# Four attention layers on one core: engine orders from a list schedule, self-attention pairs between cross pairs, the 8-bit layer's clamps on GpSimd and its takes on two engines, x loaded first

## Chip, cores, metric

One core of a Trainium2 chip. The time is that of one execution of the program on the device, in microseconds (us); the median of several runs is used for comparisons. TensorE (PE) runs at a granted clock: 1.00 in the profile is 2.4 GHz, 0.50 is 1.2 GHz.

## What is computed

`x` is 32 sequences of 112 tokens of 256 channels, `ctx` is 32 sequences of 375 tokens of 256 channels. Four layers follow one another on x, each attending to ctx with 16 heads, everything in float32:

```python
x = L0(x, ctx)   # rmsnorm of x and of ctx, cross-attention, 4 key/value heads of 64, residual
x = L1(x, ctx)   # layer norm, self-attention, layer norm, cross-attention, gated FFN (exact gelu);
                 # heads of 16; q, k, v and the softmax weights rounded to 8 bits:
                 #   xq = clip(round(x / delta) + zp, 0, 255); (xq - zp) * delta
x = L2(x, ctx)   # layer norm, cross-attention, 16 heads of 64, FFN of 1024 (relu)
x = L3(x, ctx)   # layer norm, causal self-attention, cross-attention, FFN of 1024; heads of 16
```

## The kernel before

**Tiling.** Channels lie on the partitions, tokens along the free axis. A *stream* is two sequences (224 tokens); a layer has 16 streams. A stream's x is read from DRAM into one of five buffers at the start of a layer and stored at its end; contexts come one sequence at a time into two buffers. All weights of a layer lie in SBUF.

**Attention.** A *unit* is one head of cross-attention (112 x 375 scores) or four heads of self-attention (112 x 448). A *pair* is two units; an *octet* is four cross pairs (eight heads of a sequence) or two self pairs (all sixteen heads). Layers 0 and 2 have 256 cross pairs; layers 1 and 3 have 256 cross and 64 self pairs. A pair goes through these steps:

- scores: PE, line 937, into two of four PSUM banks; waits for the exp of the pair two before
- max: DVE, line 1215; in layer 1 also the product with a scale, nmaxc, line 1219
- exp: ACT, line 1106, one instruction (and one read of its sum) for each unit, or for each head in a self unit; writes `e`, which holds four pairs, so it waits for the turns of the pair four before
- invert: DVE, line 1226; in layer 1 also rsumw, line 1230
- weigh: POOL (GpSimd), lines 1431 (layer 1) and 1434, in place in `e`
- turn: PE transposes, line 950 (cross) and 947 (self), into a bank of the ring
- take: a copy from PSUM to `probs`, on DVE (1295) or ACT (1120); in layer 1 always DVE (1293), where it takes off the rounding constant and applies the bound 255
- pv: PE, lines 975, 982, 989, 964, once for an octet; its save is DVE's.

**Jobs.** Every other matrix product is a *job*: norms (mean, var), q, k, v, context keys and values (ck, cv), output products (o, o2), FFN (f1, gate, up, f2). Jobs, turns and pvs use a ring of four PSUM banks in the order of PE's queue; job n waits for the save of job n - 4. The products run from line 1000. In layer 1 a quantised product (q, k, v, ck, cv; 16 a stream) is saved by ACT (line 1142: scaled and rounded, into one of four tiles of `work`), clamped by DVE (line 1264) and, right behind it and with a wait for it, unpacked by DVE (*clip*, lines 1271 to 1282). ACT's save of product n waits for the clip of product n - 4.

**Order of work.** A Python planner (`Plan`) writes out every engine's queue before the program is built. Each step has a hand-given *position*, counted in pairs: a turn comes 2.35 positions after its scores (2.85 for self-attention), an FFN job so many after its stream's last pair. `arrange` sorts PE's steps by position and keeps that order; a running clock with estimated costs then gives every other step a due time, and DVE, ACT, POOL and SP execute theirs sorted by due time. A step marked "VA" goes to whichever of DVE and ACT is free earlier. All queues run in order, tied by semaphores. In layers 1 and 3 the self pairs of stream s + 1 stand among the cross pairs of stream s as whole octets: self, cross, self, cross, cross, cross, so two self pairs follow one another.

**Start.** SP loads constants, four vectors of parameters and the causal mask, then (by due time) the three weight parts that are free at once (3.25 MB of layer 0, layer 1's early part and layer 2's v), then x, two contexts and so on. DVE makes scales and masks (lines 1368 to 1400) in a chain; ACT waits for it (`setup_done`) before its first instruction on data.

## Time and profile before

| what | value |
|---|---|
| median of 3 runs | 5542.59 us (5533.66 to 5542.77) |
| the profiled execution, its own time | 5541.59 us |
| its span, first to last instruction | 5539.8 us |
| mean granted clock of PE | 0.957 |
| instructions | 90952 |

In the page's 40 slices PE's granted clock is lowest in slices 9 to 18 and PE's busy share in slices 1 and 8 to 18:

```profile
PE   8999999888888888889999999999999999999999
...
PEclk9999999988888888889999999999999999999999
```

Each digit is a tenth of a slice of 138.5 us; 9 is 90% or more. Layer 0 runs to about 990 us, layer 1 to 2490, layer 2 to 4150, layer 3 to the end. A busy PE is not a PE at its peak: matmul ends are modelled. An engine's idle time costs nothing where the engine isn't what the end waits for.

### The profile page before, as it was taken

The page shows a single profiled execution, that of the slowest core. Times are in us where ns is not written, and L with a number is a line of the kernel's source. Part 1 is how long each engine was busy: PE and PEld are TensorE (multiplying, and loading weights), DVE is VectorE, ACT ScalarE, POOL GpSimd, SP SyncE. Part 2 cuts the span into 40 slices and gives each one's busy share as a digit, 9 for nine tenths or more (in the row PEclk, how much of TensorE's full clock was granted, in tenths as well). Part 3 has the DMA queues.
Part 4 walks back from the last instruction along what each step waited for, and adds up shares of the span by engine and source line. Part 5 has one row for each costly group of instructions (what it writes and reads, how often), then busy time and mean ns, then how long its engine had stood idle before and what let it go on. Part 6 is the DMA issues. An engine that isn't in the chain of part 4 may idle for free.

```text
span 5539.8 us, 90952 instructions
## 1 busy us (share of the span) xinstructions
PE 5246.6 (95%) x34496; PEld 3760.9 (68%) x34496; DVE 3463.5 (63%) x7972; ACT 2652.3 (48%) x8353; POOL 1559.0 (28%) x3090
## 2 busy tenths in 40 slices
PE   8999999888888888889999999999999999999999
PEld 5666666566667676666666666666677777777777
DVE  5555555677777777775455555555556666666665
ACT  4555555666665666653232232223234555555554
POOL 2332322333332323332111111111113333333332
PEclk9999999988888888889999999999999999999999
DMA  1000000100000000000100000000000100000000
GB/s 71 19 19 25 21 19 17 43 13 10 19 10 16 13 10 19 10 31 14 36 13 10 15 12 10 16 12 10 14 21 19 36 16 13 19 19 11 19 18 9
DMA packets 39746, 103.05 MB, mean 19 GB/s; under 512 B 4880, under 2 KB 21520, under 8 KB 38032
## 3 DMA queue, kind: packets, MB, share of 16 engines
q1 hardware_dynamic: 39312, 97.23, 5.3%
q8 instruction: 276, 4.52, 0.3%
q14 instruction: 158, 1.29, 0.1%
HBM read 82.53 MB, written 14.68 MB: 18 GB/s over the span
## 4 chain that ended last, share of the span: by engine, by line
PE 83%; DVE 8%; ACT 5%; POOL 2%; issue 1%; DMA 0%; SPq 0%; ACTq 0%
PE ring L1000 49%; PE score L937 13%; PE ring L950 11%; ACT e L1106 3%; PE ring L982 3%; PE ring L975 3%; DVE nmax L1215 3%; PE ring L947 2%; PE ring L989 1%; DVE probs L1293 1%; POOL e L1431 1%; POOL e L1434 1%; DVE nmaxc L1219 1%; PE ring L964 1%; DVE values L1282 1%
## 5 line engine op out<-in xcount | busy, mean ns | idle before, releaser
L1434 POOL TENSOR_SCALAR e<-e,rsum 112x375 f32<-112x375 f32 (+1 forms) x2048 | 1065.9, 536 | 2922.7 <-DVE rsum L1226 2921.3
L1106 ACT ACTIVATE e<-score,nmax 112x375 f32<-112x375 f32 (+1 forms) x2048 | 1041.1, 528 | 655.6 <-DVE nmax L1215 651.9
L1215 DVE TENSOR_REDUCE nmax<-score 112x2 f32<-112x750 f32 (+1 forms) x1152 | 1099.1, 954 | 325.3 <-PE score L937 312.2
L950 PEld LDWEIGHTS ring<-consts,e 112*125 112x125 f32 x6144 | 821.1, 192 | 328.7 <-issue 188.6
L950 PE MATMUL ring<-consts,e 112*125 112x112 f32 x6144 | 920.1, 284 | 84.3 <-POOL e L1431 41.5
L1000 PE MATMUL ring<-h,weights 128*128 128x224 f32 x3840 | 951.1, 377 | 16.6 <-ACT h L1084 12.8
L1000 PEld LDWEIGHTS ring<-h,weights 128*128 128x128 f32 x3840 | 708.5, 199 | 166.7 <-issue 62.4
L937 PE MATMUL score<-keys,q 64*112 64x375 f32 (+2 forms) x3584 | 788.0, 505 | 2.7 <-DVE q L1271 1.1
L1431 POOL TENSOR_SCALAR e<-e,rsumw 112x375 f32<-112x375 f32 (+1 forms) x1024 | 480.8, 488 | 1027.3 <-DVE rsumw L1230 1026.4
L1106 ACT ACTIVATE e<-score,nmaxc,quant 112x375 f32<-112x375 f32 (+1 forms) x1024 | 555.3, 564 | 367.7 <-DVE nmaxc L1219 367.0
L1120 ACT COPY probs<-ring 125x336 f32<-125x336 f32 (+1 forms) x716 | 301.0, 440 | 729.6 <-PE ring L950 718.4
L1000 PE MATMUL ring<-weights,ctx 128*125 128x256 f32 (+1 forms) x1536 | 570.2, 502 | 0.5 <-DVE probs L1293 0.5
L1000 PE MATMUL ring<-ctx,weights 128*128 128x375 f32 x1536 | 559.7, 486 | 9.5 <-DVE work L1345 6.8
L1295 DVE COPY probs<-ring 125x336 f32<-125x336 f32 (+1 forms) x948 | 471.1, 517 | 91.0 <-PE ring L950 72.0
L937 PEld LDWEIGHTS score<-keys,q 64*112 64x112 f32 (+2 forms) x3584 | 245.4, 165 | 331.8 <-issue 249.1
L1106 ACT ACTIVATION_READ_ACCUMULATOR e<-score,nmax 112x1 f32 x2048 | 438.4, 214 | 0.0
L1000 PE MATMUL ring<-work,weights 128*128 128x224 f32 (+1 forms) x1792 | 403.9, 374 | 2.4 <-DVE work L1251 1.7
L1000 PE MATMUL ring<-heads,weights 128*128 128x224 f32 x1536 | 367.6, 386 | 31.1 <-ACT work L1142 30.7
L1000 PEld LDWEIGHTS ring<-ctx,weights 128*128 128x128 f32 x1536 | 275.2, 191 | 174.6 <-issue 57.0
L1000 PEld LDWEIGHTS ring<-weights,ctx 128*125 128x125 f32 x1536 | 284.4, 192 | 149.5 <-issue 104.0
L1000 PEld LDWEIGHTS ring<-work,weights 128*128 128x128 f32 x1792 | 328.1, 190 | 44.8 <-issue 8.2
L1000 PEld LDWEIGHTS ring<-heads,weights 128*128 128x128 f32 x1536 | 301.8, 205 | 79.8 <-ACT work L1142 33.8
(105 smaller groups left out, 5193.7 us busy)
## 6 DMA issues: line engine op xcount, KB each, us to landing
ctx<-ctx_t SPq DMA_DIRECT2D x128, 375.0 KB, 3.0
out_t<-x SPq DMA_DIRECT2D x64, 224.0 KB, 2.0
x<-out_t SPq DMA_DIRECT2D x48, 224.0 KB, 3.2
weights<-weights SPq DMA_DIRECT2D x5, 1024.0 KB, 4.8
x<-x_t SPq DMA_DIRECT2D x16, 224.0 KB, 3.2
weights<-weights SPq DMA_DIRECT2D x1, 3328.0 KB, 10.9
weights<-weights SPq DMA_DIRECT2D x1, 2560.0 KB, 8.8
weights<-weights SPq DMA_DIRECT2D x1, 2304.0 KB, 9.1
```

Of the source, the lines that this page charges most:

```text
L937: ins = pe.matmul(score_bank(u)[0:S, n * width:(n + 1) * width], lhs, rhs, start=not masked, stop=not masked or n == nt - 1)
L947: ins = pe.transpose(dst[0:S, n * S:(n + 1) * S], src[:, n * S:(n + 1) * S], idt[0:S, 0:S])
L950: ins = pe.transpose(dst[0:R, c * S:(c + 1) * S], src[:, c * R:(c + 1) * R], idt[0:S, 0:S])
L975: ins = pe.matmul(ps[64 * odd:64 * odd + 64, 0:4 * S], vs[0:R, c, kv:kv + 64], probs_of(o, c, 4 * odd, 4 * S), start=c == 0, stop=c == last)
L982: ins = pe.matmul(ps[64 * odd:64 * odd + 64, i * S:(i + 1) * S], vs[0:R, c, hd:hd + 64], probs_of(o, c, 4 * odd + i, S), start=c == 0, sto ...
L1000: ins = pe.matmul(out_, a, b_, start=n == 0, stop=n == len(parts) - 1)
L1106: ins = nc.scalar.activation(e_of(u)[:, n * width:(n + 1) * width], score_bank(u)[0:S, n * width:(n + 1) * width], ACT.Exp, bias=minus, sc ...
L1120: ins = nc.scalar.copy(dst, src)
L1215: ins = dve.tensor_reduce(to, src, AX, ALU.max, negate=True)
L1295: ins = dve.tensor_copy(dst, src)
L1431: ins = nc.gpsimd.tensor_scalar(mine, mine, rsumw[0:S, slot(u), n:n + 1], ROUND, ALU.mult, ALU.add)
L1434: ins = nc.gpsimd.tensor_scalar(mine, mine, rsum[0:S, slot(u), n:n + 1], 0.0, ALU.mult, ALU.add)
```

## The change

1. **Orders.** Every step on PE (T), DVE (V), ACT (A), POOL (G) and SP's queue (D) becomes a `Step` with a cost, a position and a list of what must come before. `arrange` plays the program through: whenever an engine is free it takes, of its steps whose inputs are done, the one with the smallest position. PE may take only steps up to 6 positions past its first open one, and no job while the ring is full. That order is written into the queues. Semaphore counts follow from it (`nth`).
2. **Self pairs** stand singly between the cross pairs of the first two cross octets: c s c s c c, twice. Turns come 2.2 positions after their scores for both kinds, pvs 0.5 after that (0.9 before, with 2.35 and 2.85).
3. **Layer 1's clamps** move from DVE to POOL, in the order ACT save, POOL clamp, DVE clip; the clip waits for `clamped` and is no longer chained to an instruction before it.
4. **Layer 1's takes** may go to ACT (Identity with bias -ROUND) as well as DVE (subtract ROUND, without the minimum). For this the bound 255 goes to the weighing, and the rounding constant is added in a second pass of POOL over the same `e`, one instruction a unit, which waits for the first pass; turns wait for it (`gridded`).
5. **nmaxc and rsumw** become products of two tensors (with `scales`, filled at setup) in place of a tensor and a per-partition scalar. Setup has three more instructions for each of two sets, and two more memsets on POOL.
6. **Start.** Layer 0's weights come in three parts (q; k and v; o), with positions after x's; the early parts of layers 1 and 2 no longer go first.

```diff
-    (0, ("q", "k", "v", "o"), 0),
+    (0, ("q",), 0),
+    (0, ("k", "v"), 2048),
+    (0, ("o",), 3072),
...
-                for at, o in zip(places, own):
-                    cross.insert(at, o)
-                for o in cross:
-                    self.octet(*o)
+                    places = (0, 1)
+                for i, o in enumerate(cross):
+                    o = self.octet(*o)
+                    beside = self.octet(*own[places.index(i)]) if own and i in places else None
+                    for n in range(4):
+                        self.pair(o)
+                        if beside and n < 2:
+                            self.pair(beside)
...
+            self.add("weigh", p, "G", (2.7 if own else 1.15) + ((1.3 if own else 1.1) if q else 0), p.index + 1.0)
...
+                self.add("clamp", j, "G", 0.55 if j.kind in ("ck", "cv") else 0.4, j.pos + 0.3)
+                self.add("clip", j, "V", self.clip_cost(j), j.pos + 0.5)
...
+            first = {0: -10.5, 1: -10.9, 2: -4.0, 3: 20.0}.get(i, 60.0)
+            self.add("weights", i, "D", 8.0, max((j.pos for j in js), default=first) + 0.3)
...
+    def arrange(self):
+        engines = ("T", "V", "A", "G", "D")
...
+        while left:
+            for e in engines:
+                if free[e] > now:
+                    continue
...
+                if e == "T":
...
+                    full = len(self.ring) >= RING and self.ring[-RING] not in released
+                    open_ = [w for w in waiting["T"] if w.pos <= undone[behind].pos + AHEAD
+                             and not (full and w.kind == "job")]
+                else:
+                    open_ = waiting[e] + (waiting["VA"] if e in "VA" else [])
+                if open_:
+                    step = min(open_, key=place)
...
+                step.end = now + cost
+                free[e] = now + (0.3 if e == "D" else cost)
+                self.order[e].append((step.kind, step.x))
...
+                events += [(free[e], serial, None), (step.end + 0.1, serial + 1, step)]
...
+                if layer == 1:
+                    rows = S if is_own(j.of.octet) else R
+                    ins = nc.scalar.activation(dst, src, ACT.Identity, bias=minus_magic[0:rows, :])
...
-                        ins = dve.tensor_scalar(nmaxc[0:S, pair_slots(p), 0:nt], to, quant[0:S, a + 4:a + 5], None, ALU.mult)
+                        ins = dve.tensor_tensor(nmaxc[0:S, pair_slots(p), 0:nt], to, scale_of(o, 0), ALU.mult)
...
-            chained(dve.tensor_scalar(r, r, ROUND + 127.0, ROUND - 128.0, ALU.min, ALU.max))
...
-                    ins = dve.tensor_scalar(dst, src, ROUND, 255.0, ALU.subtract, ALU.min)
+                    ins = dve.tensor_scalar(dst, src, ROUND, None, ALU.subtract)
...
+                if kind == "clamp":
+                    rows, width = quantised_shape(x_)
+                    r = rounded[0:rows, x_.place % 4, 0:width]
+                    wait.saves([x_])
+                    nc.gpsimd.tensor_scalar(r, r, ROUND + 127.0, ROUND - 128.0, ALU.min, ALU.max).then_inc(clamped, 1)
+                    continue
...
-                            ins = nc.gpsimd.tensor_scalar(mine, mine, rsumw[0:S, slot(u), n:n + 1], ROUND,
-                                                          ALU.mult, ALU.add)
+                            ins = nc.gpsimd.tensor_scalar(mine, mine, rsumw[0:S, slot(u), n:n + 1], 255.0,
+                                                          ALU.mult, ALU.min)
...
+                if o.layer == 1:
+                    wait.wait_ge(weighed, nth["weigh", p])
+                    for u in p.units:
+                        mine = e_of(u)[:, 0:count_of(o) * width]
+                        ins = nc.gpsimd.tensor_scalar(mine, mine, ROUND, 0.0, ALU.add, ALU.add)
+                    ins.then_inc(gridded, 1)
```

## Rows read from the trace of the kernel before

**Rows 1.** The page's part 1: busy us of each engine (share of the span) and instructions.
```profile
PE 5246.6 (95%) x34496; PEld 3760.9 (68%) x34496; DVE 3463.5 (63%) x7972; ACT 2652.3 (48%) x8353; POOL 1559.0 (28%) x3090
```

**Rows 2.** Busy time by stage: stretch, length, engines, granted clock, DMA share, GB/s.
```profile
0.00:25.00 25.00, 4.41 (x9) 3.09 (x10) 7.73 (x38) 3.56 (x6) 2.65 (x9) 1.00 0.73 283
25.00:990.00 965.00, 963.15 (x5024) 612.10 (x5023) 547.53 (x1107) 504.60 (x1496) 287.14 (x497) 1.00 0.07 21
990.00:2490.00 1500.00, 1265.56 (x8260) 992.95 (x8260) 1135.60 (x3099) 917.77 (x2680) 485.11 (x1027) 0.85 0.05 16
2490.00:4150.00 1660.00, 1656.57 (x9594) 1124.67 (x9594) 859.47 (x1679) 510.40 (x1532) 295.91 (x514) 1.00 0.05 16
4150.00:5500.00 1350.00, 1326.36 (x11397) 1001.27 (x11400) 901.41 (x2025) 708.93 (x2626) 484.45 (x1038) 1.00 0.06 18
```

**Rows 3.** The same view: one repeat of layer 1 and its stretches at 0.50.
```profile
1606.55:1702.12 95.57, 80.91 (x529) 64.26 (x530) 72.33 (x199) 58.74 (x170) 30.04 (x64) 0.84 0.04 14
1606.55:1623.62 17.07, 10.61 (x61) 7.47 (x61) 11.55 (x31) 10.08 (x41) 7.79 (x21) 0.50 0.07 23
1637.27:1644.10 6.83, 6.45 (x40) 4.32 (x39) 5.31 (x15) 6.41 (x25) 2.09 (x7) 0.50 0.00 0
1661.17:1668.00 6.83, 6.21 (x19) 5.77 (x20) 4.80 (x16) 3.68 (x10) 2.33 (x4) 0.50 0.00 0
```

**Rows 4.** Waits of PE, 990 to 2490 us: total us, times, longest us.
```profile
PE ring L947 <- POOL e L1431: 53.3, 17, 3.5
PE ring L950 <- POOL e L1431: 41.5, 47, 2.3
```

**Rows 5.** The chain of waits, 1606 to 1625 us: start us, us, what.
```profile
1608.90 2.34 ACT e L1106 x11
...
1614.82 2.70 POOL e L1431 x8
...
1617.66 1.71 PE ring L947 x8
```

**Rows 6.** Groups of instructions: busy us, mean ns of one, idle before; POOL's by form.
```profile
L1431 POOL TENSOR_SCALAR e<-e,rsumw 112x375 f32<-112x375 f32 x512 | 304.6, 607 | 816.3 <-DVE rsumw L1230 816.0
L1431 POOL TENSOR_SCALAR e<-e,rsumw 112x112 f32<-112x112 f32 x512 | 176.8, 368 | 211.0 <-DVE rsumw L1230 210.4 <-DVE rsum L1226 0.6
...
L1215 DVE TENSOR_REDUCE nmax<-score 112x2 f32<-112x750 f32 (+1 forms) x1152 | 1099.1, 954 | 325.3 <-PE score L937 312.2
L1106 ACT ACTIVATE e<-score,nmax 112x375 f32<-112x375 f32 (+1 forms) x2048 | 1041.1, 528 | 655.6 <-DVE nmax L1215 651.9
L1293 DVE TENSOR_SCALAR probs<-ring 125x336 bf16<-125x336 f32 (+1 forms) x640 | 315.5, 525 | 46.0 <-PE ring L947 36.6 <-PE ring L950 6.7
L1120 ACT COPY probs<-ring 125x336 f32<-125x336 f32 (+1 forms) x716 | 301.0, 440 | 729.6 <-PE ring L950 718.4 <-PE ring L947 9.9
L1264 DVE TENSOR_SCALAR work<-work 128x224 f32<-128x224 f32 (+4 forms) x256 | 85.6, 334 | 92.6 <-ACT work L1142 92.3
```

**Rows 7.** Waits of PE, 4150 to 5500 us.
```profile
PE ring L947 <- POOL e L1434: 19.4, 15, 1.4
```

**Rows 8.** The timeline of the start: start us, us, instruction, idle before it.
```profile
3.53 1.38 SPq L1477 DMA_DIRECT2D weights<-weights  x3
4.96 0.50 SPq L1457 DMA_DIRECT2D x<-x_t  x1
...
13.14 0.46 DVE L1400 TENSOR_SCALAR qbias<-vectors,qmask 128x1 f32<-128x1 f32 x2
19.87 0.58 ACT L1073 ACTIVATE squares<-x 128x448 f32<-128x448 f32 x1 [17.86 <-DMA x<-x_t]
```

**Rows 9.** The page's part 6, DMA issues: count, KB each, median us to landing.
```profile
x<-x_t SPq DMA_DIRECT2D x16, 224.0 KB, 3.2
```

**Rows 10.** Two lines of DVE: duration ns as min/median/max, first and last start us.
```profile
L1275 DVE TENSOR_SCALAR keys<-work x32: 276/552/605, 946.3 to 2333.1; 128x224 bf16<-128x224 f32 x32
...
L1219 DVE TENSOR_SCALAR nmaxc<-nmax,quant x320: 227/228/1874, 981.5 to 2527.6; 112x2 f32<-112x2 f32 x128, 112x8 f32<-112x8 f32 x32
```

More of the change, by code:

```diff
@@ L104 @@
     half: int
-    first: int = 0
-    last: int = 0
+    pairs: tuple = ()
 @dataclass(eq=False)
@@ L135 @@
     nth: int = 0
-    clip: int = 0
-    norm: int = -1
+    pos: float = 0.0
+    norm: object = None
+    place: int = 0
 @dataclass(eq=False)
@@ L149, in mm, with __init__ @@
     return count * n / 600.0
+class Step:
+    def __init__(self, kind, x, by, cost, pos):
+        self.kind, self.x, self.by, self.cost, self.pos = kind, x, by, cost, pos
+        self.then, self.left, self.end = [], 0, None
 class Plan:
@@ L205, in span, with octets_of @@
+            if p is o.pairs[-1] and len(o.pairs) == (2 if o.attn == "self" else 4):
+                self.pv_of[o] = self.job(p.index + lag + 0.5, "pv", o.layer, o.s, o.b, o.half, PV_BY, o)
+    def octets_of(self, layer, attn, s):
+        return [o for o in self.octets if (o.layer, o.attn, o.s) == (layer, attn, s)]
     def span(self, layer, attn, s):
-        os = [o for o in self.octets if (o.layer, o.attn, o.s) == (layer, attn, s)]
-        return os[0].first, os[-1].last + 1
+        os = self.octets_of(layer, attn, s)
+        return os[0].pairs[0].index, os[-1].pairs[-1].index + 1
@@ L421, in clock_of @@
         for layer in range(4):
+            for b in range(B):
+                first = [j.pos for j in self.jobs if j.layer == layer and j.b == b and j.kind in ("cvar", "ck", "cv")]
+                self.add("ctx", (layer, b), "D", 4.0, min(first) - 2.5)
             for s in range(STREAMS):
-                sync.append((one(layer, "f2" if layer else "o", s, 0, 1) + 1.0, "store", (layer, s)))
+                self.add("store", (layer, s), "D", 2.0, self.at[layer, "f2" if layer else "o", s, 0, 1].pos + 0.5)
@@ L442, in clock_of @@
                 user = (32 if layer == 1 else 128) + slot
-                j = self.products(user - VS)[-1]
-                pool.append((ends[j] + 3.0, "zero", (layer, slot, j)))
-        j = self.at[1, "pv", last, B - 1, 0]
-        own = [i for i in self.ring if i.kind == "pv" and i.layer == 1 and i.of.attn == "self"]
-        pool.append((ends[own[-1]] + 40.0, "zero_own", own[-1]))
-        self.pool = [x[1:] for x in sorted(pool, key=lambda x: x[0])]
+                self.add("zero", (layer, slot), "G", 0.8 if layer == 1 else 1.6,
+                         self.value_users(user - VS)[-1].pos + 1.0)
@@ new lines, in before_save @@
+    def before_save(self, j):
+        yield "job", j
+        if j.kind == "turn":
+            o = j.of.octet
+            if o.index >= 2:
+                yield "job", self.pv_of[self.octets[o.index - 2]]
+        elif j.kind == "mean":
+            yield from self.h_free(j.norm)
+        elif j.kind == "var":
+            if j.norm.index >= 2:
+                yield "scale", self.norms[j.norm.index - 2]
+        elif j.kind == "cvar":
+            if j.b:
+                yield "cscale", j.b - 1
+        elif not (j.layer == 1 and j.kind in QUANTISED):
+            yield from self.frees(j)
@@ new lines, in ready, with query_jobs, key_jobs, value_jobs @@
+    def ready(self, j):
+        return ("clip" if j.layer == 1 and j.kind in QUANTISED else "save"), j
+    def query_jobs(self, o):
+        return self.every(o.layer, "q2" if o.layer in (1, 3) and o.attn == "cross" else "q", s=o.s)
+    def key_jobs(self, o):
+        if o.attn == "self":
+            return self.every(o.layer, "k", s=o.s)
+        return [j for j in self.every(o.layer, "ck", b=o.b) if o.layer != 2 or j.m // 4 == o.half]
+    def value_jobs(self, o):
+        if o.attn == "self":
+            return self.every(o.layer, "v", b=o.b)
+        return [j for j in self.every(o.layer, "cv", b=o.b) if o.layer != 2 or j.m // 3 == o.half]
@@ L762, in done @@
                 self.wait_ge(job_done, max([j.index for j in jobs], default=-1) + 1)
-        every = plan.every
-        last_s = STREAMS - 1
-        turns = {j.of: j for j in plan.ring if j.kind == "turn"}
-        pv_of = {j.of: j for j in plan.ring if j.kind == "pv"}
-        def turned_input(wait, p):
-            wait.wait_ge(weighed, p.index + 1)
+        every, nth = plan.every, plan.nth
+        eight_bit = [x_ for k_, x_ in plan.order["G"] if k_ == "weigh" and x_.octet.layer == 1]
+        grid_count = {p: i + 1 for i, p in enumerate(eight_bit)}
@@ L898, in tensor_program @@
             wait.wait_ge(consts_loaded, 16)
-            wait.wait_ge(consts_made, 6)
-            for kind, x_ in plan.tensor:
+            wait.wait_ge(consts_made, 8)
+            for kind, x_ in plan.order["T"]:
                 if kind == "scores":
@@ L955, in tensor_heads @@
             layer = o.layer
-            wait.saves([turns[u] for p in plan.pairs[o.first:o.last + 1] for u in p.units])
+            wait.saves([plan.turn_of[u] for p in o.pairs for u in p.units])
+            wait.products(plan.value_jobs(o))
             last = CHUNKS - 1
             if is_own(o):
-                wait.products(every(layer, "v", b=o.b))
                 for half in range(2):
@@ L968, in tensor_heads @@
                 return ins
-            wait.products([i for i in every(layer, "cv", b=o.b) if layer != 2 or i.m // 3 == o.half])
             vs = cross_values(layer, o.b, o.half)
```

788 lines of the change are left out of this document (469 added, 319 removed).

## The prediction

> **What bounds the kernel now.** I read the page's busy line first: PE is busy 95% of the span [rows 1]. The table by stage says where the rest is [rows 2]. Layer 0 (25 to 990 us) and layer 2 (2490 to 4150 us) have PE busy for 963.15 of 965 us and 1656.57 of 1660 us at a granted clock of 1.00; no order of work can give anything there. Layer 3 has 23.6 us of PE idle time in 1350 us, the start 20.6 us. Layer 1 (990 to 2490 us) has 234 us of idle PE and a granted clock of 0.85: it pays twice, with idle time and with busy time at the lower clock. So I cut one stream's repeat of layer 1 along the clock [rows 3]. It lasts 95.57 us (the pattern comes back at this distance through the layer, so 1500 us are 15.7 repeats). PE is busy 80.91 us, of which 10.61 + 6.45 + 6.21 = 23.27 us lie in the three stretches at 0.50 (1.2 GHz). At 2.4 GHz those would be about 11.6 us, so PE's own work is 57.6 + 11.6 = 69.3 us. The difference, 26 us in each repeat or 410 us in all, is the most that layer 1 can give.
>
> Why PE stops: its waits in layer 1 are led by the turns (transposes) of weighed scores, on POOL [rows 4]. The chain through the largest gap shows what feeds it [rows 5]: two self-attention pairs in a row put sixteen exps on ACT (a piece of eleven of their instructions takes 2.34 us), then come eight weighings on POOL (2.70 us), and only then does PE turn. No other engine is full in this repeat: DVE 72.3 us, ACT 58.7, POOL 30.0 of 95.6 [rows 3]. It is latency in a fixed order, made worse by bunching, and by the clock that falls when PE has starved.
>
> **The change, part by part, for one repeat of layer 1** (16 cross pairs, 4 self pairs, 16 quantised products).
>
> PE: not one matmul is added or removed. 69.3 us stays.
>
> POOL: the weighing is now two passes, the second being one instruction per unit: 32 of 375 wide and 8 of 448 wide. A 375-wide one takes 0.607 us, a 112-wide one 0.368 [rows 6]; the line through both gives 0.67 us at 448. So 32 x 0.607 + 8 x 0.67 = 24.8 us. The clamps are 16 instructions of 224 to 512 wide, which the same line puts at 0.47 to 0.73 us: about 8.7 us. Each second pass also waits for the first to drain, which no row shows; between 0 and 0.3 us (the largest gap between two engines in the chain is 0.2), I take 0.15, so 3 us for 20 pairs. POOL goes from 30.0 to about 66.5 us.
>
> DVE: the clamps go, 85.6 us / 16 = 5.3 us [rows 6]. nmaxc and rsumw are still 40 small instructions, with two tensors in place of a tensor and a scalar: no cost taken; bounds below. 72.3 - 5.3 = 67 us. ACT stays at 58.7. The takes (315.5 us / 16 = 19.7 us for 40, all DVE's now) may go to either; a copy of such a tile costs ACT 0.440 us, and that is the price I take there [rows 6]. Shared evenly, (67 + 58.7)/2, both carry about 63 us, with some 9 takes moved.
>
> So at the floor of 69.3 us PE would be full and three engines 90% to 96% full. Four in-order queues don't all run at that. The orders are worked out from estimated costs in which an engine hears of another's end after 0.1 us. The self pairs are split up, which takes the bunch out of ACT and POOL, and PE may choose among steps up to six positions ahead, so most of the 14.7 us of idle time should go. But a self pair's weighing grows from 2.7 to some 4.2 us, and a cross pair's from 1.2 to 2.4 us, on the very path PE waits for. The bounds are 69.3 us (all gained) and 95.6 us (nothing). Layer 3 keeps PE 98% busy, but with DVE at 67%, ACT 53% and POOL 36% [rows 2]; layer 1 before has 85% with DVE at 76%. I take 88% to 90% of PE's 69.3 us, 78 us, and 2 us for stretches still at 1.2 GHz: **80 us a repeat**. 15.7 x 15.6 = **245 us gained**.
>
> Layers 0 and 2: 5.3 us of PE idle in 2625 us. The new order can only lose here. A pair there takes 965/256 = 3.8 us and 1660/256 = 6.5 us of PE, so a turn 2.2 positions later comes 8 or 14 us after its scores, and the chain (maximum 0.95, two exps 1.1 and the last of their sums, two weighings 1.2 [rows 6], five handovers of up to 0.2) is under 5 us: it is covered. I take 5 us lost, bounds 0 and 40 (1.5%).
>
> Layer 3: 19.4 of its 23.6 us of PE waiting are turns of self pairs on POOL [rows 7]. Spreading these pairs removes the bunch, but the turn's distance for self pairs falls from 2.85 to 2.2. I take 12 us gained, bounds 24 gained and 15 lost.
>
> Start: the first x is issued at 4.96 us behind three weight transfers, and its square starts at 19.87 us [rows 8]. With x issued first, at about 3.5 us, and landing 3.2 us later [rows 9], the bound becomes the vector constants: the setup ends at 13.6 us now, and ACT waits for it [rows 8]. Six more links of about 0.25 us each make 15.1 us. Gain 19.9 - 15.3 = 4.6, say 5 us, if the weights for q (1 MB, behind x, context and k, v) are down by 19 us. Bounds 0 and 6. The tail, from the last pair to the store, is a chain of single steps: unchanged. What else is moved on SP's queue (loads, stores and the weights now in 13 parts for 11) comes in a stage whose DMA share is 0.04 to 0.07 [rows 2], and I take nothing for it.
>
> Sum: 245 - 5 + 12 + 5 = 257 us. The profiled execution took 5541.59 us (span 5539.8, 1.8 us around it), the median of the runs is 5542.59, 1 us more. 5541.6 - 257 = 5284.6; I forecast **5285 us**.
>
> **Rivals.**
> (A) PE is nearly filled. Repeat of 70 to 75 us, nothing left at 1.2 GHz. For it: each loop has buffers for it (four pairs in e, two in score banks). Against: three other engines over 85%. Gain 20.6 to 25.6 x 15.7 = 323 to 402 us, plus 12: 5130 to 5207 us. Chance 0.15.
> (B) DVE and POOL get in each other's way. The row that speaks for it: the clips of k take 276 ns at best and 552 ns at the median, the same instruction on the same shape, with POOL busy 31% of this time, and nmaxc reaches 1874 ns over a median of 228 [rows 10]. Against: for nmaxc the median is the minimum plus 1 ns. If about 76 DVE instructions a repeat (40 small products, 30 clips, 6 scalings) meet a POOL busy at 85% and wait for half of a 0.6 us instruction, that is 76 x 0.85 x 0.3 = 19 us. DVE carries 82 us, and the repeat becomes 87 to 92 us: gain 55 to 135 us, plus 12; 5395 to 5475 us. Chance 0.15. The Trainium skill, in SBUF — State Buffer, "Who interferes with whom", says that a DVE instruction with two SBUF inputs, as the new nmaxc and rsumw are, or in a two-port mode, shuts out a GpSimd instruction that reads SBUF and the reverse, for the whole instruction. By that rule this case, not mine, is to be expected; the medians there agree with it for one kind of clip alone.
> (C) Slower. ACT's queue is held by POOL's. ACT may save quantised product n only when product n - 4 is clipped, and that now needs POOL's clamp, which can stand behind a weighing of 4.2 us. Behind the waiting ACT stand all exps. Sixteen such waits a repeat at 2.5 us would bring ACT to 63 + 40 = 103 us: 7.4 x 15.7 = 116 us lost, 5650 us. It decides from (95.6 - 63)/16 = 2.0 us a wait. Against: the new order puts a save only after its clip is due. Chance 0.06.
> (D) The fixed order, built from estimates, mismatches the chip everywhere: all layers lose 1% to 2%, layer 1 gains little; near 5540 us. Chance 0.04.
>
> **How the numbers follow.** Forecast 0.60, A 0.15, B 0.15, C 0.06, D 0.04. The forecast's own range is a repeat of 76 to 86 us with the bounds of the other terms: 5210 to 5390. To leave out no more than 0.2 it takes in half of A and of B: **5180 to 5430**. Slower by more than 0.2% (11 us, about what a measurement of this kernel can tell from none): C and half of D, 0.08; within 0.2%: 0.02; faster: 0.90.
>
> **What would show it.** A repeat near 80 us in layer 1 with PE busy about 90% and a clock near 0.95; POOL busy about 1560 + 16 x 33.5 = 2095 us in all; DVE and ACT within 5 us of each other per repeat; layers 0 and 2 at 965 and 1660 us; first matmul near 16 us. Wrong if POOL's mean 375-wide instruction is far over 0.61 us or nmaxc's far over 0.25 us (B), if ACT waits for clips (C), or if layers 0 and 2 grow by more than 40 us (D).

## The result and the profile after

The changed kernel takes 6382.18 us (median of 4 runs, 6378.09 to 6382.93) against 5542.51 us before: the ratio is 1.1516, 95% interval 1.1502 to 1.1531. It is slower by 15%, where 5285 us was forecast and 5180 to 5430 us was the range.

The page of the changed kernel, its part 1 and the lines of its part 2 for POOL and for PE's clock:

```profile
PE 5495.3 (86%) x34496; PEld 3941.6 (62%) x34496; DVE 3168.4 (50%) x7302; ACT 2840.8 (45%) x8773; POOL 3344.2 (52%) x3988
...
POOL 2333337999999999999994111111111233333333
PEclk9999997677777777777769999999999999999999
```

Against [rows 1], DVE has 295 us less to do and POOL 1785 us more. POOL executes 898 instructions more, 640 of the second pass, 256 clamps and two memsets, as the change lays them out; but its busy time was to be about 2095 us. In slices 8 to 21 POOL is full. The table by stage (columns as in [rows 2]):

```profile
0.00:25.00 25.00, 8.02 (x27) 5.95 (x28) 11.66 (x50) 6.16 (x10) 2.74 (x11) 1.00 0.86 323
25.00:990.00 965.00, 961.66 (x5048) 615.81 (x5047) 529.02 (x1075) 514.30 (x1533) 317.17 (x510) 1.00 0.07 20
990.00:3390.00 2400.00, 1546.34 (x8407) 1186.23 (x8405) 964.77 (x2654) 1061.65 (x2955) 2224.18 (x1915) 0.73 0.04 11
3390.00:5050.00 1660.00, 1659.28 (x9658) 1130.66 (x9660) 819.03 (x1614) 526.94 (x1590) 315.23 (x528) 1.00 0.05 15
5050.00:6340.00 1290.00, 1288.14 (x11129) 974.90 (x11126) 831.70 (x1884) 724.44 (x2666) 480.83 (x1019) 1.00 0.06 18
```

All the time was lost in layer 1, which went from 1500 to 2400 us. POOL is busy for 2224 of them, PE for 1546 and at a granted clock of 0.73 instead of 0.85. Layers 0 and 2 are as they were, and layer 3 has PE busy for 1288 of 1290 us. The groups of instructions on POOL by form (against [rows 6]) say what fills it:

```profile
L1673 POOL TENSOR_SCALAR e<-e,rsumw 112x375 f32<-112x375 f32 x512 | 807.6, 1587 | 96.7 <-DVE rsumw L1462 79.3
L1683 POOL TENSOR_SCALAR e<-e 112x375 f32<-112x375 f32 x512 | 759.6, 1499 | 22.4
L1673 POOL TENSOR_SCALAR e<-e,rsumw 112x112 f32<-112x112 f32 x512 | 331.6, 671 | 20.5 <-DVE rsumw L1462 14.8
L1683 POOL TENSOR_SCALAR e<-e 112x448 f32<-112x448 f32 x128 | 220.1, 1734 | 5.6
...
L1664 POOL TENSOR_SCALAR work<-work 128x375 f32<-128x375 f32 x64 | 32.8, 512 | 13.1 <-ACT work L1376 8.2
```

L1673 is the first pass, the same instruction on the same tiles as L1431 before, with one operation of two changed (multiply, minimum in place of multiply, add). It costs 1587 ns at 375 columns instead of 607. L1683, the second pass (add, add), costs 1499 ns where I had put 607. The clamps (minimum, maximum; L1664) cost 512 ns, less than I had put. In all, POOL works 2237 us on layer 1 (these five rows and the four other forms of the clamps), or 139.8 us a stream. The chain of waits in the middle of the layer consists of POOL and nothing else:

```profile
1699.19 3.11 POOL e L1673 x2
1702.30 0.08 issue
1702.38 2.96 POOL e L1683 x2
1705.34 0.10 issue
1705.43 3.11 POOL e L1673 x2
```

and PE waits for POOL's second pass, first for turns of cross pairs (L1184), then of self pairs (L1181):

```profile
PE ring L1184 <- POOL e L1683: 518.6, 182, 5.5
PE ring L1181 <- POOL e L1683: 206.5, 55, 7.0
```

**Where the 841 us are.** Two marks recur in every kernel: the gelu, ACT's only instruction from `heads` to `heads`, once in each of layer 1's 16 streams, and the causal mask's matmuls, from the first to the last self pair of layer 3. Their rows in the kernel before (duration ns as min/median/max, then first and last start):

```profile
L1089 ACT ACTIVATE heads<-heads x16: 1696/1697/1698, 1180.2 to 2604.3; 128x1792 f32<-128x1792 f32 x16
...
L932 PE MATMUL score<-causal_b,ident_b x128: 350/352/354, 4138.2 to 5404.8; 112*112 112x448 bf16 x128
```

and in the changed kernel:

```profile
L1320 ACT ACTIVATE heads<-heads x16: 1696/1697/1697, 1281.6 to 3475.0; 128x1792 f32<-128x1792 f32 x16
...
L1162 PE MATMUL score<-causal_b,ident_b x128: 350/352/355, 5013.2 to 6254.0; 112*112 112x448 bf16 x128
```

| stretch | before | after | difference |
|---|---|---|---|
| start to first gelu | 1180.2 | 1281.6 | +101.4 |
| first to last gelu, 15 repeats | 1424.1 (94.9 each) | 2193.4 (146.2 each) | +769.3 |
| last gelu to first mask (layer 2 within) | 1533.9 | 1538.2 | +4.3 |
| first to last mask (layer 3) | 1266.6 | 1240.8 | -25.8 |
| last mask to the end of the span | 135.0 | 127.1 | -7.9 |
| span | 5539.8 | 6381.1 | +841.3 |

The start within the first stretch went as forecast. In the timeline the first square on ACT comes at 15.54 us, 4.3 us earlier than in [rows 8], and it waits for DVE's setup now:

```profile
15.54 0.58 ACT L1304 ACTIVATE squares<-x 128x448 f32<-128x448 f32 x1 [13.53 <-DVEq L1636]
```

### The profile page after: what moved, and what is told of

It is laid out like the page before. It is cut to its first block, busy times and chain, and to the rows that moved or that the text cites. A ratio compares the mean times of both kernels' runs of the same rounds, so it can differ in the third digit from the quotient of the medians.

```text
span 6381.1 us, 91617 instructions
## 1 busy us (share of the span) xinstructions
PE 5495.3 (86%) x34496; PEld 3941.6 (62%) x34496; DVE 3168.4 (50%) x7302; ACT 2840.8 (45%) x8773; POOL 3344.2 (52%) x3988
## 4 chain that ended last, share of the span: by engine, by line
PE 62%; POOL 34%; DVE 2%; issue 1%; ACT 0%; DMA 0%; SPq 0%; ACTq 0%; DVEq 0%
PE ring L1233 34%; POOL e L1673 18%; POOL e L1683 15%; PE score L1167 11%; PE ring L1184 10%; PE ring L1215 2%; PE ring L1208 2%; PE ring L1222 1%; POOL work L1664 1%; PE ring L1181 1%; PE ring L1198 0%; PE score L1162 0%; DVE values L1512 0%; DVE rsumw L1462 0%; DVE own L1512 0%
## 5 line engine op out<-in xcount | busy, mean ns | idle before, releaser
L1184 PE MATMUL ring<-consts,e 112*125 112x112 f32 x6144 | 1041.9, 305 | 533.0 <-POOL e L1683 518.6
L1184 PEld LDWEIGHTS ring<-consts,e 112*125 112x125 f32 x6144 | 884.7, 207 | 918.9 <-issue 696.7
L1673 POOL TENSOR_SCALAR e<-e,rsumw 112x112 f32<-112x112 f32 (+1 forms) x1024 | 1139.3, 1129 | 117.2 <-DVE rsumw L1462 94.1
L1355 ACT COPY probs<-ring 125x336 f32<-125x336 f32 (+1 forms) x929 | 383.5, 444 | 1428.0 <-PE ring L1184 1383.7
L1683 POOL TENSOR_SCALAR e<-e 112x375 f32<-112x375 f32 (+1 forms) x640 | 979.7, 1546 | 28.0
L1233 PEld LDWEIGHTS ring<-h,weights 128*128 128x128 f32 x3840 | 744.4, 207 | 109.1 <-issue 38.7
L1337 ACT ACTIVATE e<-score,nmaxc,quant 112x112 f32<-112x112 f32 (+1 forms) x1024 | 553.8, 556 | 156.2 <-DVE nmaxc L1452 98.6
L1233 PE MATMUL ring<-ctx,weights 128*128 128x375 f32 x1536 | 594.3, 515 | 0.0
L1353 ACT ACTIVATE probs<-ring,minus_magic 125x336 bf16<-125x336 f32 (+1 forms) x338 | 183.4, 556 | 828.8 <-PE ring L1184 483.0
L1525 DVE COPY probs<-ring 125x336 f32<-125x336 f32 (+1 forms) x735 | 365.7, 515 | 60.4 <-PE ring L1184 48.3
```

Of the source, the lines that this page charges most:

```text
L1184: ins = pe.transpose(dst[0:R, c * S:(c + 1) * S], src[:, c * R:(c + 1) * R], idt[0:S, 0:S])
L1233: ins = pe.matmul(out_, a, b_, start=n == 0, stop=n == len(parts) - 1)
L1337: ins = nc.scalar.activation(e_of(u)[:, n * width:(n + 1) * width], score_bank(u)[0:S, n * width:(n + 1) * width], ACT.Exp, bias=minus, sc ...
L1353: ins = nc.scalar.activation(dst, src, ACT.Identity, bias=minus_magic[0:rows, :])
L1355: ins = nc.scalar.copy(dst, src)
L1525: ins = dve.tensor_copy(dst, src)
```

## The experiments

Theory 1: the price of a POOL instruction hangs on its pair of operations; multiply-minimum and add-add are slow, and they are the whole loss. Theory 2: POOL was slowed by its surroundings (a second pass over the same data, DVE's use of SBUF, as in rival B). Behind it stood the question what the new orders are worth when POOL isn't in the way.

**p1_probe: POOL's instructions by themselves.** In the kernel before, behind POOL's last weighing, each waiting for the one before it:

```diff
+            for i in range(4):
+                for w_ in (375, 112):
+                    v_, s_ = pt[:, 0:w_], probe[0:S, 600:601]
+                    g_(v_, v_, s_, 0.0, ALU.mult, ALU.add)
+                    g_(v_, v_, s_, 255.0, ALU.mult, ALU.min)
+                    g_(v_, v_, s_, 0.0, ALU.mult, ALU.max)
+                    g_(v_, v_, ROUND, 0.0, ALU.add, ALU.add)
+                    g_(v_, v_, 1.0, ROUND, ALU.mult, ALU.add)
+                    g_(v_, v_, ROUND + 127.0, ROUND - 128.0, ALU.min, ALU.max)
+                    g_(v_, v_, ROUND, 1.0, ALU.add, ALU.mult)
+                    g_(v_, v_, 2.0, 0.5, ALU.mult, ALU.mult)
+                    g_(v_, v_, ROUND, 0.0, ALU.subtract, ALU.add)
+                    g_(v_, v_, ROUND, 255.0, ALU.subtract, ALU.min)
+                    g_(v_, v_, ROUND, None, ALU.add)
```

> The kernel before with 88 more instructions on POOL behind its last weighing, on a quiet tile: eleven pairs of operations, each on 375 and on 112 columns, four times. Theory 1 (the pair of operations sets the price): at 375 columns multiply-then-add with a scalar from memory takes 0.60 us, multiply-then-minimum with the same operands about 1.59 us, add-then-add with constants about 1.50 us, minimum-then-maximum about 0.51 us, and multiply-then-add with two constants about 0.5 to 0.6 us. Theory 2 (the second pass, or DVE's new use of SBUF, slowed POOL down; the instructions as such cost the same): all eleven lie within 0.1 us of 0.60 us here, where DVE is nearly idle. Span: that of before plus about 60 to 90 us of tail.

Measured: 5571.37 us, one run, 46 us above the kernel before that ran beside it, where 60 to 90 us were expected. The first eleven instructions at 375 columns, in the order of the diff (the view of one line in narrow stretches; L1446 is the helper's line):

```profile
L1446 POOL TENSOR_SCALAR heads<-heads x1: 596/596/596, 5494.8 to 5494.8; 112x375 f32<-112x375 f32 x1
L1446 POOL TENSOR_SCALAR heads<-heads x1: 1580/1580/1580, 5495.4 to 5495.4; 112x375 f32<-112x375 f32 x1
L1446 POOL TENSOR_SCALAR heads<-heads x1: 1569/1569/1569, 5497.1 to 5497.1; 112x375 f32<-112x375 f32 x1
L1446 POOL TENSOR_SCALAR heads<-heads x1: 1517/1517/1517, 5498.8 to 5498.8; 112x375 f32<-112x375 f32 x1
L1446 POOL TENSOR_SCALAR heads<-heads x1: 525/525/525, 5500.4 to 5500.4; 112x375 f32<-112x375 f32 x1
L1446 POOL TENSOR_SCALAR heads<-heads x1: 500/500/500, 5501.0 to 5501.0; 112x375 f32<-112x375 f32 x1
L1446 POOL TENSOR_SCALAR heads<-heads x1: 523/523/523, 5501.6 to 5501.6; 112x375 f32<-112x375 f32 x1
L1446 POOL TENSOR_SCALAR heads<-heads x1: 527/527/527, 5502.2 to 5502.2; 112x375 f32<-112x375 f32 x1
L1446 POOL TENSOR_SCALAR heads<-heads x1: 1517/1517/1517, 5502.8 to 5502.8; 112x375 f32<-112x375 f32 x1
L1446 POOL TENSOR_SCALAR heads<-heads x1: 1495/1495/1495, 5504.4 to 5504.4; 112x375 f32<-112x375 f32 x1
L1446 POOL TENSOR_SCALAR heads<-heads x1: 1172/1172/1172, 5506.0 to 5506.0; 112x375 f32<-112x375 f32 x1
```

There are two prices. Multiply-add, add-multiply, multiply-multiply and minimum-maximum cost 500 to 596 ns; multiply-minimum, multiply-maximum, add-add, subtract-add and subtract-minimum cost 1495 to 1580 ns; an add alone, with one operation less, costs 1172 ns. In the other three rounds no value differs by more than 10 ns from these. These are a quiet engine's numbers, on other data, and they lie within 20 ns of those in the changed kernel's layer 1 (1580 for 1587, 1517 for 1499, 500 for 512). Theory 2 is out, and so is "more operations cost more": multiply by 1.0 and add is less than half of an add alone.

**e1_second_pass_mult_add.** One operation of the change: the second pass as multiply by 1.0, add ROUND.

```diff
-                        ins = nc.gpsimd.tensor_scalar(mine, mine, ROUND, 0.0, ALU.add, ALU.add)
+                        ins = nc.gpsimd.tensor_scalar(mine, mine, 1.0, ROUND, ALU.mult, ALU.add)
```

> The changed kernel with the second pass over e as multiply by 1.0, then add ROUND (the same result). Theory 1: a 375-wide second pass falls from 1.50 to about 0.55 us, the first pass stays at 1.59; POOL's work per repeat of layer 1 falls by 36 us, from 140 to 104, and with it the repeat from 153 to about 115: 6382 - 15.7 x 38 = 5790 us. Theory 2: nothing changes, 6380 us.

Measured: 5732.59 us (one run), 650 us less than the changed kernel. The second pass takes 519 ns at 375 columns, the first still 1577. The gelu's first and last starts are 1210.6 to 2824.9 us, 107.6 us a repeat: somewhat more was won than forecast.

**e2_first_pass_mult_add.** The other one: the first pass as multiply, add.

```diff
-  ... mine, mine, rsumw[0:S, slot(u), n:n + 1], 255.0, ALU.mult, ALU.min)
+  ... mine, mine, rsumw[0:S, slot(u), n:n + 1], 0.0, ALU.mult, ALU.add)
```

> The changed kernel with the first pass as multiply by rsumw, then add 0.0; the bound of the weights at 255 is left out. Theory 1: a 375-wide first pass falls from 1.59 to 0.60 us and a 112-wide one from 0.67 to 0.37; POOL's work per repeat falls by 41 us to 99, the repeat to about 110: 6382 - 15.7 x 43 = 5710 us. Theory 2: 6380 us.

Measured: 5726.33 us (one run), 16 us more than expected; first pass 622 ns, second 1507; 107.5 us a repeat. With one slow pass left, e1 and e2 are still slower than the kernel before.

**e3_both_passes_fast.** Both, and the bound of 255 kept: the first pass rounds, the second clamps.

```diff
-  ... rsumw[0:S, slot(u), n:n + 1], 255.0, ALU.mult, ALU.min)
+  ... rsumw[0:S, slot(u), n:n + 1], ROUND, ALU.mult, ALU.add)
...
-                        ins = nc.gpsimd.tensor_scalar(mine, mine, ROUND, 0.0, ALU.add, ALU.add)
+                        ins = nc.gpsimd.tensor_scalar(mine, mine, ROUND + 255.0, ROUND, ALU.min, ALU.max)
```

> The changed kernel with the first pass as multiply by rsumw, then add ROUND, and the second as minimum with ROUND + 255, then maximum with ROUND (the same result). Theory 1: first pass 0.60 us, second about 0.51 us at 375 columns; POOL's work per repeat about 60 us, no longer the bound; the repeat is then what was forecast, 76 to 86 us, and the kernel takes 5180 to 5350 us. Theory 2: 6380 us. A third, that the list schedule's order itself is bad in layer 1: POOL fast, but the repeat still above 95 us, 5550 us or more.

Measured: 5390.72 us, ratio to before 0.9757 (0.9741 to 0.9773). With three constants and operation names changed, on the same orders and with the same count of instructions, 991 us are gone. POOL's groups and PE's waits here:

```profile
L1673 POOL TENSOR_SCALAR e<-e,rsumw 112x375 f32<-112x375 f32 x512 | 316.2, 627 | 143.7 <-DVE rsumw L1462 133.3
L1683 POOL TENSOR_SCALAR e<-e 112x375 f32<-112x375 f32 x512 | 252.6, 509 | 22.4
```

```profile
PE score L1167 <- ACT e L1337: 100.2, 82, 3.8
PE ring L1233 <- ACT work L1376: 41.9, 25, 2.6
```

POOL works 58.2 us a repeat (930.7 us in nine groups, over 16 streams). The repeat is 88.3 us (gelu 1158.3 to 2483.5), slower than the 76 to 86 I had given and faster than the 95 of a bad order. PE's longest waits in all are now for ACT's exps. The time lies 41 us over the 5350 us that stood as the upper end for it.

**e4_before_with_slow_passes.** The opposite test: the kernel before, its own orders, with only the two slow passes.

```diff
-  ... rsumw[0:S, slot(u), n:n + 1], ROUND, ALU.mult, ALU.add)
+  ... rsumw[0:S, slot(u), n:n + 1], 255.0, ALU.mult, ALU.min)
...
+                if o.layer == 1:
+                    wait.wait_ge(weighed, p.index + 1)
+                    for u in p.units:
+                        mine = e_of(u)[:, 0:count_of(o) * width]
+                        ins = nc.gpsimd.tensor_scalar(mine, mine, ROUND, 0.0, ALU.add, ALU.add)
+                    grids[0] += 1
+                    ins.then_inc(gridded, 1)
```

> The kernel before, its orders kept, with only the weighing of layer 1 as in the change: multiply, minimum, then a second pass add, add. Theory 1 (POOL's slow pairs of operations are the whole loss): POOL's work per repeat of layer 1 is 132 us and the repeat 140 to 155 us, so 6240 to 6480 us, about as slow as the changed kernel. A rival, that the new orders made a slow POOL worse: clearly under 6240 us.

Measured: 6486.07 us (one run), 148.4 us a repeat (gelu 1317.3 to 3543.0), 6 us above the range expected. The two slow passes alone do it, with the old orders as with the new.

The next runs take the change apart with POOL's fast pairs.

**e5_one_pass_takes_on_dve.** Clamps on POOL, orders, spread pairs and start as in the change; one pass (multiply, add ROUND) and the takes on DVE with their minimum, as before.

```diff
+  ... "turn", o.layer, o.s, o.b, 0, "V" if o.layer == 1 else "VA", u)
...
-            self.add("weigh", p, "G", (2.7 if own else 1.15) + ((1.3 if own else 1.1) if q else 0), p.index + 1.0)
+            self.add("weigh", p, "G", (2.7 if own else 1.15), p.index + 1.0)
...
-                    ins = dve.tensor_scalar(dst, src, ROUND, None, ALU.subtract)
+                    ins = dve.tensor_scalar(dst, src, ROUND, 255.0, ALU.subtract, ALU.min)
...
-  ... rsumw[0:S, slot(u), n:n + 1], 255.0, ALU.mult, ALU.min)
+  ... rsumw[0:S, slot(u), n:n + 1], ROUND, ALU.mult, ALU.add)
...
-                if o.layer == 1:
-                    wait.wait_ge(weighed, nth["weigh", p])
...
-                    ins.then_inc(gridded, 1)
```

> The changed kernel with the weighing of layer 1 as it was (one pass, multiply then add ROUND), its takes on DVE alone with the minimum there, and the clamps on POOL; orders from the list schedule. POOL's work per repeat falls from 60 us in the run with both passes fast to 38, ACT's by the takes, DVE carries 67. If the second pass and ACT's takes cost more than they give: repeat under 88.7 us, about 82, 5290 us. If DVE's takes were the better thing to move: over 88.7 us, 5400 us or more.

Measured: 5352.39 us, ratio 0.9658 (0.9642 to 0.9674), 85.6 us a repeat (gelu 1154.0 to 2437.8). It leaves nothing out (the takes apply the bound of 255) and is faster than both kernels.

**e6_orders_alone.** e5 with the clamps back on DVE, chained to their clips: before's work, the change's orders. The two-tensor products of the change's fifth part stay, and so do the spread pairs and the start.

```diff
-                self.add("clamp", j, "G", 0.55 if j.kind in ("ck", "cv") else 0.4, j.pos + 0.3)
-                self.add("clip", j, "V", self.clip_cost(j), j.pos + 0.5)
+                self.add("clip", j, "V", self.clip_cost(j) + 0.38, j.pos + 0.5)
...
+            chained(dve.tensor_scalar(r, r, ROUND + 127.0, ROUND - 128.0, ALU.min, ALU.max))
```

> The engines' work of the kernel before (clamps and takes of layer 1 on DVE, one pass of weighing) with the list schedule's orders, the spread self pairs and x first. If the orders carry the gain: DVE at 72 us a repeat, repeat 82 to 88 us, 5300 to 5400 us. If moving work off DVE carries it: repeat above 92 us, 5450 us or more.

Measured: 5449.41 us, ratio 0.9830 (0.9816 to 0.9845), 91.4 us a repeat (gelu 1173.5 to 2543.9), between the two cases. What e6 keeps of the change gives 94 us. In the traces 54 us of it lie between the first and the last gelu, and 34 us behind layer 3's first mask (4082.2 to the end of the span at 5450.2, 1368.0 us for 1401.6). The two-tensor products, of the same results, take DVE 131 us for 155 in this run (forms added up); what they give of the 54 us wasn't separated from the orders. The clamps' move gives another 97 us (5449.4 to 5352.4; the two share their chip and their runs of before), more than the 85.6 us that they are busy on DVE [rows 6]: the repeat is 5.8 us shorter, and POOL had room.

**e7_self_pairs_as_octets.** e3 with whole octets of self pairs.

```diff
-                    places = (0, 1)
-                for i, o in enumerate(cross):
-                    o = self.octet(*o)
...
-                        if beside and n < 2:
-                            self.pair(beside)
+                    places = (0, 2)
+                for at, o in zip(places, own):
+                    cross.insert(at, o)
+                for o in cross:
+                    o = self.octet(*o)
+                    for n in range(2 if o.attn == "self" else 4):
+                        self.pair(o)
```

> The run with both passes fast, but the self pairs as whole octets between cross octets, as before (self, cross, self, cross, cross, cross). If spreading them matters: two self pairs in a row bunch on ACT and POOL again, repeat of layer 1 at 91 to 95 us, 5430 to 5500 us. If the list schedule's choice by readiness does it all: within 15 us of 5391 us.

Measured: 5402.5 us, ratio 0.9748 (0.9733 to 0.9762), against 0.9757 (0.9741 to 0.9773) for e3: no difference that can be told: the medians lie 12 us apart, but the two ran beside different runs of before (5542.96 and 5525.02 us). Its repeat is 90.1 us (gelu 1157.4 to 2508.4) against 88.3, and layer 3's masks run from 4036.5 to 5269.0, 1232.5 us, as fast as with spread pairs. The spreading was worth at most 1.8 us a repeat in layer 1 by these traces, one of each, and nothing in layer 3.

**e9_one_pass_takes_on_two.** The changed kernel with one pass and the takes on both engines; the bound of 255 is left out.

```diff
-            if o.layer == 1:
-                wait.wait_ge(gridded, grid_count[p])
...
+            wait.wait_ge(weighed, nth["weigh", p])
...
-  ... rsumw[0:S, slot(u), n:n + 1], 255.0, ALU.mult, ALU.min)
+  ... rsumw[0:S, slot(u), n:n + 1], ROUND, ALU.mult, ALU.add)
...
-                        ins = nc.gpsimd.tensor_scalar(mine, mine, ROUND, 0.0, ALU.add, ALU.add)
-                    ins.then_inc(gridded, 1)
```

> The changed kernel with one pass of weighing (multiply, add ROUND) and the takes of layer 1 on DVE and ACT; the bound of the weights at 255 is left out. Against the run with both passes fast (5391 us) this takes away the second pass alone; against the run with the takes on DVE (5352 us) it adds ACT's takes alone. If the second pass is what made the former 38 us slower: 5340 us or less. If ACT's takes are: 5375 us or more.

Measured: 5382.58 us, ratio 0.9711 (0.9696 to 0.9725), 88.2 us a repeat (gelu 1153.8 to 2476.3). Against e5, whose interval it doesn't touch and whose runs of before agree within 1 us, ACT's takes cost 30 us. What the second pass costs is less sure: e3 is 8 us slower by the medians and 25 us by the ratios (0.9757), as its runs of before were faster; the repeats, 88.3 and 88.2, are alike. The busy times from the first to the last gelu (columns as in [rows 2]), first e5:

```profile
1154.00:2437.80 1283.80, 1149.79 (x7892) 934.75 (x7891) 983.97 (x2708) 813.61 (x2365) 551.11 (x1123) 0.92 0.06 17
```

then e9:

```profile
1153.80:2476.30 1322.50, 1178.23 (x7915) 956.20 (x7914) 879.81 (x2424) 941.66 (x2650) 536.06 (x1122) 0.88 0.06 17
```

In e5 DVE is busy 77% and ACT 63%; in e9, 67% and 71%. The second looks better balanced and is slower. Of the 2.6 us a repeat 0.7 us are more idle time of PE and 1.9 us more busy time for the same matmuls, at a granted clock of 0.88 for 0.92. One would think that a take ahead of an exp in ACT's queue delays PE's next scores, but the waits don't show that. In e5 PE waits (1000 to 2350 us)

```profile
PE score L1167 <- ACT e L1334: 103.2, 82, 2.9
```

and in e9

```profile
PE score L1167 <- ACT e L1334: 77.5, 63, 3.1
PE ring L1195 <- ACT work L1373: 25.7, 13, 2.0
PE ring L1181 <- POOL e L1670: 15.3, 17, 1.1
PE ring L1219 <- ACT rdev L1361: 14.1, 13, 1.2
```

The waits for exps fell, and waits for ACT's other steps and for POOL came up. That moving takes to ACT costs time is shown; by which wait, is not.

**e8_one_pass_exp_costs, e10_both_passes_exp_costs, e11_one_pass_ahead_10.** Is it the planner's estimates, or its window, that keep the repeat over 80 us?

```diff
-            self.add("exp", p, "A", 2.9 if own else 1.3, p.index + 0.5)
+            self.add("exp", p, "A", 3.4 if own else 1.4 if q else 1.3, p.index + 0.5)
...
-AHEAD = 6.0
+AHEAD = 10.0
```

The first edit is e8 on e5; with a take of 0.6 us it is e10 on e3. The second is e11 on e5.

> The run with one pass of weighing and the takes on DVE, with the planner's estimate for a self pair's exps at 3.4 us in place of 2.9 (eight exps of 0.42 us are measured) and for a layer-1 cross pair's at 1.4 in place of 1.3. If PE's 103 us of waits of scores for exps come from orders made for an ACT faster than the chip's: these waits fall by half or more, the repeat from 85.6 to 81 to 83 us, 5290 to 5320 us. If they are ACT's load itself: within 10 us of 5352 us.

> The run with both passes fast (5391 us) with the planner's exp costs as above and a take in layer 1 at 0.6 us in place of 0.5. If wrong cost estimates hold the repeat of layer 1 at 88.4 us: 5320 to 5360 us. If the load on four engines does: within 10 us of 5391 us.

> The run with one pass of weighing and the takes on DVE (5352 us, repeat 85.6 us), with PE allowed to take steps up to 10 positions ahead in place of 6. If PE stops because its window holds nothing that is ready: the waits for exps turn into other work, the repeat falls to 82 us or less, 5300 us. If it stops on scores that the fixed order has placed too early for the chip: within 10 us of 5352 us.

Measured: e8 5348.13 us, ratio 0.9649 (0.9635 to 0.9663), the same as e5, with 112.8 us of PE's scores waiting for exps (103.2 in e5); e10 5429.64 us, 0.9797 (0.9780 to 0.9813), slower than e3; e11 5386.11 us, 0.9727 (0.9711 to 0.9743), slower than e5. e8's repeat is 85.3 us. In e11 the waits for exps did halve,

```profile
PE score L1167 <- ACT e L1334: 52.6, 68, 4.1
PE ring L1181 <- DVE h L1527: 33.1, 12, 2.9
PE ring L1195 <- DVE work L1572: 32.4, 12, 2.7
```

but others took their place. All three expectations of a gain fell. Truer estimates don't make better orders here; why e10's came out worse (39 us by the medians, 22 by the ratios) stays open.

## Why the prediction was wrong

**What bounds before:** right. Only layer 1 and the small remainders could move, and only they moved.

**POOL's term: the step that failed.** "A 375-wide one takes 0.607 us ... 32 x 0.607 + 8 x 0.67 = 24.8 us" priced the second pass by an instruction with other operations, and the sentence gave the first pass no new price at all, though its second operation changed from add to minimum. Measured: first pass 71.2 us a stream (807.6 + 331.6, over 16) for 30.0, second 61.2 for 24.8, clamps 7.4 for 8.7. POOL's 66.5 us became 139.8, more than any other engine's, and the repeat of 80 us became 146.2. The direction, too, hangs on this alone: e3 changes nothing else and is 2.4% faster than before. The row that I leaned on was for the same engine, tile and width; what differed was the pair of operations. With the other ends that the rows allowed (none showed a minimum or a lone add on POOL) the bound upward was open, and I closed it with the straight line.

**No rival held it.** B put POOL's trouble in the port shared with DVE and priced DVE's delay at 19 us; C put it in ACT's queue. POOL full by its own work was not among them. The prediction's sign "POOL's mean 375-wide instruction is far over 0.61 us" did appear, but it had been written down for B. C's sign did not: ACT's saves of the quantised products (L1376) waited for PE alone, 212.9 us in all, and never for a clip.

**Rival B itself.** After the change, with POOL full in layer 1, the clips of context keys and the two-tensor product look like this (columns as in [rows 10]):

```profile
L1508 DVE TENSOR_SCALAR keys<-work x64: 343/357/2036, 1006.5 to 3301.0; 128x375 bf16<-128x375 f32 x64
...
L1452 DVE TENSOR_TENSOR nmaxc<-nmax,scales x320: 162/164/516, 975.5 to 3399.6; 112x2 f32<-112x2 f32 x158, 112x8 f32<-112x8 f32 x2
```

and the same product in e3, where POOL's pairs are fast:

```profile
L1452 DVE TENSOR_TENSOR nmaxc<-nmax,scales x320: 162/211/534, 976.2 to 2408.1; 112x2 f32<-112x2 f32 x158, 112x8 f32<-112x8 f32 x2
```

The medians of the changed kernel hide it, but the blocking that B named does happen. In the timeline of e5, POOL's weighing ends at 1205.89 + 1.15 = 1207.04 us, and a product that began meanwhile ends with it, at 1207.05, after 0.55 us instead of 0.16:

```profile
1205.89 1.15 POOL L1670 TENSOR_SCALAR e<-e,rsumw 112x375 f32<-112x375 f32 x2
...
1206.50 0.55 DVE L1449 TENSOR_TENSOR nmaxc<-nmax,scales 112x2 f32<-112x2 f32 x1
```

With the fast pairs this is the rule. Of e3's 640 such products (nmaxc and rsumw), 285 began with at least 0.19 us of a POOL instruction left, and 279 of these ended within 40 ns of its end. With the slow pairs of the changed kernel it is not: of 463 such products one did, 143 took more than 30 ns over the minimum, and 319 took no longer than that. Why the slow pairs let them through stays open. The fast case agrees with the Trainium skill, SBUF — State Buffer, "Who interferes with whom": a DVE instruction with two SBUF inputs waits for a GpSimd instruction that reads SBUF to end. The slow case does not agree with it, and here the measurement decides.

The price is small either way. Over the minimum of 162 ns, e3's products take 57 us more in all of layer 1, 3.6 us a repeat, where B had put 19 us on DVE. Before the change the 640 products took 155 us, in the changed kernel 127, in e3 161: the two-tensor form, 162 ns for 227 at its quickest, which I had put at no gain, gives DVE nothing where it is blocked this often. That e3's repeat of 88.3 us lies in B's range of 87 to 92 is chance, as DVE is busy 61.4 us of it and not 82.

**The repeat of 80 us:** mis-sized even with POOL's fast pairs. It is 88.3 us in e3 and 85.6 with the changed orders in e5, so layer 1 gives 6.6 to 9.3 us a repeat where I took 15.6. The stretches from the first to the last gelu say which term it was. Before, then e3 (e5 and e9 stand above):

```profile
1180.20:2604.30 1424.10, 1221.89 (x7888) 960.55 (x7886) 1061.26 (x2874) 846.88 (x2422) 434.25 (x905) 0.85 0.05 15
...
1158.30:2483.50 1325.20, 1162.58 (x7904) 938.22 (x7903) 920.87 (x2436) 941.69 (x2640) 827.69 (x1693) 0.91 0.05 16
```

Divided by 15 repeats, with PE's own work at the prediction's 69.3 us (an estimate from [rows 3]; the matmuls are the same):

| us a repeat | before | forecast | e3 | e5 | e9 |
|---|---|---|---|---|---|
| PE idle | 13.5 | 8.7 | 10.8 | 8.9 | 9.6 |
| PE busy beyond 69.3 | 12.2 | 2 | 8.2 | 7.4 | 9.2 |
| repeat | 94.9 | 80 | 88.3 | 85.6 | 88.2 |
| granted clock | 0.85 | near 0.95 | 0.91 | 0.92 | 0.88 |

The idle time came near the forecast. The term that failed is the "2 us for stretches still at 1.2 GHz": it is 7 to 9 us, since the idle time that is left still comes with a clock well under 0.95. The even load came out as I wanted it, 62.8 us on ACT and 61.4 on DVE in e3, though by other numbers: the planner gave ACT 21 takes a stream, not 9, at 556 ns, not 440. My step "The takes ... may go to either ... Shared evenly, ... both carry about 63 us" counted that as free; e9 against e5 shows that it costs 30 us.

**Spread self pairs:** that splitting them "takes the bunch out of ACT and POOL" is not shown to be worth anything; e7 is level with e3.

**Layer 3:** 12 us forecast, bound 24; 33.7 us came from the first mask to the end (25.8 + 7.9), beyond the bound. PE's 19.4 us of waits for POOL [rows 7] are gone, and so is nearly all other idle time of PE. e7 has the gain (1368.1 us for 1401.6) without the spread pairs, so it comes from the list schedule and the new distances of the turns. It also shows that the tail is "unchanged": 135.6 us from its last mask to the end, for 135.0 before. In the changed kernel this stretch is 127.1 because the spread pairs move the last mask, with 948 matmuls recorded behind it and not 1036. The bound counted idle time alone. In e7 PE is idle 23.7 us less behind the first mask and busy 9.9 us less with as many matmuls (11689 recorded for 11690), at a granted clock of 1.00 for 0.99; how much of the 9.9 us is the clock stays open.

**Start:** 5 us forecast, 4.3 came, by the step described: the setup chain is the bound now. **Layers 0 and 2:** 5 us lost forecast; 4.3 us in the stretch around layer 2, and PE busy 961.66 of 965 us in layer 0's. **Second pass's drain:** 0.15 us taken; the chain shows 0.08 to 0.10.

## What to carry to other kernels

Price a changed instruction by a row with the same operations, not only the same engine and shape; where none exists, its upper bound is open, and a probe of a few instructions behind the kernel's end settles it in one run. When work moves between engines, even loads are no aim in themselves: with 30 us at stake, the less even split was the faster one here. Where the clock falls with idle time, count what it costs as a term of its own, from a stretch measured at such a share of idle time; here it was three quarters of the idle time and more. Read the mean beside the median: a wait that strikes a quarter of the instructions doesn't show in the median. An engine at 30% has room for work that is priced right: here the clamps, as minimum-maximum, went to POOL for 97 us.

## What the runs showed of the hardware

- POOL's tensor_scalar on float32 has two prices by the pair of operations. From 112 to 375 columns, multiply-add rises from 362 to 596 ns, 0.89 ns a column; multiply-minimum from 691 to 1580 ns, 3.4 ns a column; minimum-maximum from 281 to 500, 0.83 ns a column.
- A lone add (1172 ns) costs more than twice multiply-by-one-and-add (525 ns) with the same result.
- With PE starved more often, its granted clock in layer 1 went from 0.85 to 0.73, and PE was busy 223 us longer for the same 15 repeats between the first and the last gelu (1445.19 for 1221.89 us).
- DVE's small product of two tensors took 162 ns at its quickest, that of a tensor and a per-partition scalar 227 ns. With POOL on fast pairs (e3), 279 of the 285 two-tensor products that began well before the end of a POOL instruction ended with it; with POOL on slow pairs (the changed kernel), 1 of 463.
